# Four transformer blocks on one core: probs times V in joint units, a timed order for layer 0, a fused tail

## The reference, cut to what matters

```
x: (4, 512, 256) float32; cond: (4, 256)
layer 0: x += proj(attn(film(rmsnorm(x))));  one head of 256;  x += mlp(film(rmsnorm(x)))
layer 1: 16 heads of 16, q and k normalised to length 1 and scaled; adaptive shift, scale and gates
layer 2: 16 heads, layernorm with adaptive shift, scale and gates
layer 3: 16 heads, layernorm, adaptive gamma and beta; x += proj(attn); out = x + ln(x)*gamma + beta, no mlp
mlp: 256 -> 1024, gelu, -> 256
```

## Time and profile before

| what | us |
|---|---|
| median of 3 runs | 1274.11 |
| lowest and highest | 1271.5, 1274.75 |
| the profiled execution, its own time | 1271.56 |
| its span in the trace | 1269.8 |
| busy: PE, DVE, ACT, POOL | 1146.6, 779.8, 834.5, 538.0 |

### The profile page before, as it was taken

How to read it: one execution, slowest core, us unless ns; L and a number is a source line. 1 busy time by engine, 2 the same in 40 slices (tenths; PEclk the granted TensorE clock), 3 DMA queues, 4 the chain that set the end, 5 groups by cost and what they waited for, 6 DMA issues and landing times.

```text
span 1269.8 us, 20478 instructions
## 1 busy us (share of the span) xinstructions
PE 1146.6 (90%) x6868; PEld 718.8 (57%) x6868; DVE 779.8 (61%) x1587; ACT 834.5 (66%) x1471; POOL 538.0 (42%) x484
## 2 busy tenths in 40 slices
PE   4879889658999899899999999999999999999993
PEld 2667767634565465555664655656656656545532
DVE  4342332657558558658567467486674765888863
ACT  2563627315776766777876868678868687687771
POOL 2454447500444433443445545335544354354143
PEclk8989999858999999999999998999999999999987
DMA  6010000050430320332312423123331232242400
GB/s 213 9 34 1 26 1 17 1 96 5 101 80 26 67 57 12 61 74 43 60 26 47 89 63 70 34 45 69 63 52 34 36 61 52 44 92 46 82 26 17
DMA packets 40999, 64.52 MB, mean 51 GB/s; under 512 B 11816, under 2 KB 26920, under 8 KB 40896
## 3 DMA queue, kind: packets, MB, share of 16 engines
q1 hardware_dynamic: 40896, 63.21, 24.5%
HBM read 22.90 MB, written 2.12 MB: 20 GB/s over the span
## 4 chain that ended last, share of the span: by engine, by line
PE 66%; DVE 12%; issue 6%; ACT 6%; POOL 4%; SPq 4%; DMA 2%; ACTq 0%; POOLq 0%; DVEq 0%
PE ring L557 11%; PE AVB L644 11%; PE ring L631 10%; PE ring L558 10%; PE ring L559 10%; PE ring L621 5%; DVE m L1043 4%; SPq L519 3%; DVE stats L950 2%; PE ring L594 2%; PE ring L669 2%; PE ring L664 2%; POOL gT_l L1125 2%; ACT probs L812 1%; POOL X L1164 1%
## 5 line engine op out<-in xcount | busy, mean ns | idle before, releaser
L1043 DVE TENSOR_REDUCE m<-ring 128x1 f32<-128x512 f32 x768 | 480.7, 680 | 110.3 <-PE ring L621 92.0
L812 ACT ACTIVATE probs<-ring 128x512 f32<-128x512 f32 x768 | 406.3, 612 | 188.2 <-PE ring L621 163.0
L621 PE MATMUL ring<-SK,SQ 48*128 48x512 f32 x768 | 299.8, 471 | 25.6 <-DMA SK<-kl 16.4
L631 PE MATMUL ring<-SQ,SK 49*128 49x512 f32 x768 | 273.6, 448 | 13.2 <-DMA SQ<-cT 4.4
L631 PEld LDWEIGHTS ring<-SQ,SK 49*128 49x128 f32 x768 | 128.5, 190 | 226.2 <-issue 91.7
L644 PE MATMUL AVB<-probs,V 128*32 128x512 f32 x1536 | 211.2, 618 | 0.8 <-issue 0.8
L1125 POOL TENSOR_TENSOR gT_l<-gT_f,gT_h 128x512 fp32r<-128x512 f32 x96 | 122.1, 1287 | 155.5 <-ACT gT_h L877 152.5
L621 PEld LDWEIGHTS ring<-SK,SQ 48*128 48x128 f32 x768 | 131.2, 192 | 64.3 <-ACT probs L812 38.7
L1120 POOL TENSOR_TENSOR postT_l<-postT_f,postT_h 128x512 fp32r<-128x512 f32 x56 | 71.5, 1282 | 150.6 <-ACT postT_h L860 74.5
L557 PE MATMUL ring<-w_h,gT_h 128*128 128x256 f32 x384 | 110.5, 288 | 1.9 <-POOL gT_l L1125 0.9
L558 PE MATMUL ring<-w_l,gT_h 128*128 128x256 f32 x384 | 107.0, 279 | 0.0
(11 more groups left out here) (154 smaller groups left out, 2002.3 us busy)
## 6 DMA issues: line engine op xcount, KB each, us to landing
SQ<-qh SPq DMA_DIRECT2D x192, 64.0 KB, 2.3
SK<-kh SPq DMA_DIRECT2D x192, 64.0 KB, 2.3
SQ<-ql SPq DMA_DIRECT2D x96, 64.0 KB, 2.3
SK<-kl SPq DMA_DIRECT2D x96, 64.0 KB, 2.3
raw<-in_w SPq DMA_DIRECT2D x20, 256.0 KB, 2.8
...
```

The source lines that it names most:

```text
L621: mm = pe.matmul(o[:, :], SQ[a % 4][r:r + KS, n // 2, c * P:(c + 1) * P], SK[a % 4][r:r + KS, n // 2, :], start=True, stop=True)
L631: mm = pe.matmul(o[:, :], SK[a % 4][r:r + KS + 1, n // 2, c * P:(c + 1) * P], SQ[a % 4][r:r + KS + 1, n // 2, :], start=True, stop=True)
L812: act.activation(probs[:, n % PROBS, :], bank(kind, a, i)[:, :], ACT.Exp, scale=SCALE[layer(unit_job(a))]).then_inc(done["scores"], 1)
L1043: nc.vector.tensor_reduce(m16[:, a % 2, col:col + 1], bank(kind, a, i)[:, :], AX_X, ALU.max, negate=True).then_inc(done["max"], 1)
```

## The change

It rewrites the making of the list and some steps:

- Two ticks form one unit of the list. PAIR (layers 1 and 2) and PAIR_LAST (layer 3) say how: p6 is the next six of the 16 products, A both `av` steps of the two ticks before, 0 and 1 the rest of the first and of the second tick. A `shift` stands ahead of the rest of its tick.
- `probs` has 12 slots; `qk` lies over `gT_h`, with waits (READ_BEFORE) of gelu for the last q or k transposes and of qktok for the last fc2.
- Layer 0 and the step to layer 1 get a time for every step too (SINGLE, SINGLE3, FFN0, FFN2, FFN3, FIRST, LEAD_IN, MAXIMA); in the step, hT2, fc1 and fc2a of job 3 stand among LEAD_IN and MAXIMA, and its fc2 at ticks 0.9 and 1.95 of the first window. The times of the other tables are moved by up to 2 ticks.
- At the start (EARLY) DVE makes high and low of the three `split_qkv` and the low part of hT1 of job 0; 12 matmuls on a constant tile (WARM) stand ahead of all work of PE.
- Low parts of oT2 and av0: ACT writes the rounded value only, DVE makes the low part from PSUM in one instruction.
- proj of layers 0 and 3 (`direct`): POOL adds the bias to X ahead of it (`bias`), DVE adds PSUM to X.
- Last job: oT2, proj and bn_stats go by halves of the tokens; `base` (POOL) and `centre` (DVE) are new, and `final` is one DVE instruction per tile. In layer 3 the sum column of V is 16, so the scale of 1/16 goes with the reciprocal.

```diff
-PROBS = 8
+PROBS = 12
-CUT = (6, 6, 6, 8, 6, 8, 8, 6, 6, 4, 4, 2, 8, 6, 2, 4)
-CUT_LAST = (6, 6, 4, 6, 4, 2, 4, 6, 2, 4, 4, 4, 4, 8, 6, 8)
+SINGLE = {"stat1": (-17.1,), "norm1": (-15.95,), "hT1": (-9.6, -9.24), "q": (-7.06, -3.56), "k": (-6.4, -3.25),
+          "v": (1.2, 3.47), "scores0": (0.36, 0.71, 1.78, 2.13), "soft0": (2.49, 2.84, 3.56, 3.91),
+          "pT0": (7.11, 7.47, 7.82, 8.48), "av0": (11.53, 12.19), "proj": (12.96, 13.21), "stat2": (13.97,),
+          "norm2": (14.93,), "bias": (1.5,)}
+FFN0 = {"hT2": (17.07, 17.17), "fc1": (20.72, 21.08, 21.43, 21.79, 24.53, 24.89, 26.67, 27.02), "gelu": (22.14, 27.38),
+        "fc2a": (25.76, 26.11), "fc2": (30.12, 32.28)}
+LEAD_IN = {"stat1": (-17.86,), "norm1": (-16.36,), "hT1": (-12.27, -11.62), "qktok": (-9.69, -9.55, -8.95, -8.51),
+           "qkss": (-9.39, -9.15, -8.71, -8.47), "qkroot": (-8.22,), "v": (-7.78, -6.6), "qkrs": (-7.93,),
+           "qknorm": (-7.49, -7.34, -7.19, -6.95), "q": (-6.46, -6.12), "k": (-6.31, -6.02),
+           "stack": (-5.87, -5.72, -5.58, 2.2)}
+MAXIMA = (-5.2, -4.55, -4.53, -4.38, -4.24, -4.23, -4.09, -3.67, -3.53, -3.38, -3.23, -3.09, -2.79, -2.5, -2.35, -2.2, -1.32, -1.23, -1.23, -1.13, -1.04, -0.74, -0.39, -0.25)
+SHIFT = -1.42
+FFN3 = {"hT2": (7.93, 8.27), "fc1": (10.07, 10.22, 10.36, 10.51, 13.94, 14.09, 14.24, 14.39), "gelu": (10.66, 14.53),
+        "fc2a": (12.33, 13.21), "fc2": (16.9, 17.95)}
+PAIR = ("p6 A p6 0 p4 1", "p6 A p6 0 p4 1", "p6 A p6 0 p6 1", "p6 A p6 0 p4 1", "p6 A p6 0 p4 1", "p6 A p6 0 p4 1", "p6 A p6 0 p6 1", "p6 A p6 0 p4 1")
+PAIR_LAST = ("p6 A p8 0 p4 1", "p6 A 0 p4 1", "p6 0 1 A", "0 p6 A p6 1", "p6 A p6 0 p4 1", "A p6 0 p2 1", "p6 A p6 0 p4 1", "p4 0 p6 1 A")
...
+def multi_window(w, work):
...
+    for t in range(0, TICKS, 2):
+        pairs, rest = [], []
+        for x in (t, t + 1):
...
+            shift = [("shift", u - 1, 0)] if v % TT == 0 and u - 1 < UNITS * JOBS else []
+            rest.append(shift + [s for at, s in work if x <= at - TICKS * w < x + 1])
+        n = TICKS * w + t
+        av = [("av", x // TT, x % TT) for x in (n - 2, n - 1)] if n > TICKS * BATCH else []
+        plan += in_order((PAIR if layer(w) < LAYERS - 1 else PAIR_LAST)[t // 2], pairs, av, rest)
...
+            pe.wait_ge(warm_ready, 1)
+            for _ in range(WARM):
+                pe.matmul(ring[RING - 1][:, :], SK[0][:, 0, 0:P], SK[0][:, 0, :], start=True, stop=True)
...
-                    for dst in (postT_f[:, i, :], postT_h[:, i, :]):
-                        ins = act.activation(dst, bank(kind, a, i)[:, :], ACT.Identity,
-                                             bias=colv[:, 0, C_V + i:C_V + i + 1])
-                    ins.then_inc(hi_in[kind], 1)
+                    act.activation(postT_h[:, i, :], bank(kind, a, i)[:, :], ACT.Identity,
+                                   bias=colv[:, 0, C_V + i:C_V + i + 1]).then_inc(hi_in[kind], 1)
...
+                elif kind in ("oT2", "av0"):
+                    dve.wait_ge(hi_in[kind], nth(kind, a, i))
...
+                        ins = nc.vector.scalar_tensor_tensor(out=postT_l[:, i, :], in0=bank(kind, a, i)[:, :],
+                                                             scalar=colv[:, layer(a), C_V + i:C_V + i + 1],
+                                                             in1=postT_h[:, i, :].bitcast(F32), op0=ALU.add, op1=ALU.subtract)
...
+                elif kind == "final" and a == JOBS - 1:
+
+                    dve.wait_ge(done["centre"], i + 1)
+                    dve.wait_ge(rstd2, nth("stat2", a))
+                    dve.wait_ge(done["base"], i // 2 + 1)
+                    nc.vector.scalar_tensor_tensor(out=tok2[:, i, :], in0=tok2[:, i, :], scalar=rstd[:, 1, i:i + 1],
+                                                   in1=tmp[:, i, :], op0=ALU.mult, op1=ALU.add).then_inc(final_dve, 1)
...
+                elif kind == "proj" and direct(a) and a < JOBS - 1:
...
+                    nc.vector.tensor_tensor(x, bank(kind, a, i)[:, :].rearrange("p (t d) -> p t d", t=2), x, ALU.add
+                                            ).then_inc(done[kind], 1)
```

More of the change, by code:

```diff
@@ new lines @@
+ATTN = {"oT1": (17.35, 17.51, 17.52, 17.53), "oT2": (18.25, 18.61), "proj": (19.15, 19.9), "stat2": (21.0,),
+        "norm2": (22.5,)}
+FFN = {"hT2": (23.6, 23.91), "fc1": (25.15, 25.16, 25.17, 25.18, 29.5, 29.51, 29.52, 29.53), "gelu": (25.19, 29.54),
+       "fc2a": (27.95, 29.5), "fc2": (30.8, 31.35)}
+FFN3 = {"hT2": (7.93, 8.27), "fc1": (10.07, 10.22, 10.36, 10.51, 13.94, 14.09, 14.24, 14.39), "gelu": (10.66, 14.53),
+        "fc2a": (12.33, 13.21), "fc2": (16.9, 17.95)}
+OUTPUT = {"gatefix": (17.9,), "final": (22.6, 24.0, 26.55, 28.8), "store": (24.45, 27.05, 28.85, 32.0), "bias": (17.95,)}
@@ new lines, in timed @@
+def timed(table, j):
+    return [(TICKS * j + at, (kind, UNITS * j + i if kind == "stack" else j, 0 if kind == "stack" else i))
+            for kind, times in table.items() for i, at in enumerate(times)]
+def around(j):
+    if not multi(j):
+        return [s for s in timed(SINGLE if j < BATCH - 1 else SINGLE3, j) if s[1] not in FIRST] + timed((FFN0, FFN0, FFN2, FFN3)[j], j)
+    steps = timed(LEAD_IN, j) if j == BATCH else timed(COSINE if layer(j) == 1 else QKV, j)
+    if j == JOBS - 1:
+        return steps + timed(LAST, j)
+    return steps + timed(ATTN, j) + timed(FFN if layer(j) < LAYERS - 1 else OUTPUT, j)
@@ new lines, in lead_in, with layer_steps @@
+def lead_in():
+    u = UNITS * BATCH
+    steps = [(TICKS * BATCH + at, ("max", u + n // 16, n % 16)) for n, at in enumerate(MAXIMA)]
+    return steps + [(TICKS * BATCH + SHIFT, ("shift", u, 0))]
+def layer_steps(l):
+    if l == 0:
+        return [(at, s) for table in (FIRST, NEXT1) for s, at in table.items()]
+    steps = []
+    for kind, times in (FOR_LAYER if l < LAYERS - 1 else FOR_LAST).items():
+        ahead = kind in ("load_mod", "modrow", "mod", "load_gate", "load_qkv", "split_qkv")
+        for i, at in enumerate(times):
+            if kind not in ("modrow", "mod", "load_mod") or i < mod_rows(l + 1):
+                steps.append((TICKS * BATCH * l + at, (kind, BATCH * l + i, 0) if kind in ("gatecast", "vones") else (kind, l + ahead, i)))
@@ L252 @@
     if _s[0] in ("proj", "fc2a", "fc2"):
+        if _s[0] == "proj" and direct(_s[1]):
+            continue
         _tiles = (2 * _s[2], 2 * _s[2] + 1)
@@ L257 @@
 PIECES = [s for s in PLAN if s[0].startswith("split")]
+EARLY = [("split_qkv", 0, i) for i in range(3)] + [("hT1", 0, i) for i in range(CH)]
+WARM = 12
+READ_BEFORE, _read, _other = {}, {}, False
+for _s in PLAN:
+    if _s[0] in ("gelu", "qktok") and _s[2] == 0:
+        READ_BEFORE[_s] = _read.get("fc2" if _s[0] == "qktok" else "q")
+        assert _read.get("open", _s[0]) == _s[0], _s
+        _read["open"] = _s[0]
+    if _s[0] == "fc2":
+        _read["fc2"] = _s
+    if _s[0] in ("q", "k") and layer(_s[1]) == 1 or _s == ("modrow", 0, 1):
+        _read["q"] = _s
+    if _s[0] == "fc2" and _s[2] == 1 or _s[0] in ("q", "k") and _s[2] == 1 and layer(_s[1]) == 1 and _other:
+        _read.pop("open", None)
+    if _s[2] == 1 and _s[0] in ("q", "k"):
+        _other = not _other
 def nth(kind, a, i=0):
@@ L549, in claim @@
                     k, b, m = USES[n - RING]
-                    freed = {"proj": y1, "fc2a": done["fc2a"], "fc2": y2, "scores0": exp0}.get(k, hi_in.get(k))
-                    pe.wait_ge(done[k] if freed is None else freed, nth(k, b, m))
+                    if k == "proj" and not direct(b):
+                        pe.wait_ge(y1, nth(k, b, m) - 2 * BATCH)
+                    else:
+                        freed = {"hT1": hi_in["hT1"], "hT2": hi_in["hT2"], "fc2": y2, "scores0": exp0}.get(k, done.get(k))
+                        pe.wait_ge(freed, nth(k, b, m))
                 return ring[n % RING]
@@ L713, in _ @@
             for kind, a, i in PLAN:
-                if kind.startswith("split"):
+                if kind.startswith("split") and (kind, a, i) not in EARLY:
                     n = PIECES.index((kind, a, i))
```

352 lines of the change are left out of this document (165 added, 187 removed), and 7 rows, old and new, of tables (FIRST, START).

## The result

The changed kernel takes **1267.25 us** (median of 20 runs, 1260.99 to 1271.43), beside 1272.95 for 20 runs of the kernel before. The ratio is **0.9956**, 95% interval [0.9944, 0.9968]: faster by 0.4%. I had predicted 1186 (1148 to 1232). The direction held and the size did not: 5.7 us came where 87 were expected.

The account below looks back on a forecast made before the run. The prediction took PE to set the end nearly everywhere, in four different ways. Its terms summed to -88, so 1183.6 us for the profiled execution and, with 2.6 for the median, 1186 (own range 1165 to 1208; stated with the result as 1148 to 1232).

Parts of the forecast that it names:

- the shift's wait: Layers 1 to 3: with fewer products behind the shift, its DMA chain falls short by up to 2 us; +8 us.
- Start and tail: Start: shorter wait for the first hT_l, -5 us; tail: fewer passes and work by halves, -9 us (-5 to -12).
- Layer 0, -18: Layer 0: PE's waits for norm2 before hT2 go nearly whole, clock gains 4, 2 given back; -5 to -28 us.
- The step and the first window: Step to layer 1 and its first window: moved mlp work 15, wait before q 4, clock 8; -27 us (-10 to -45).
- the first rival: Whole kernel: evacuation by ACT and DVE is the bound, work leaving PE returns as waits; 1227 us, chance 0.25.
- Joints, -16: Layers 1 and 2: 64 joins of two `av` save 0.25 us each; -16 us (0 to -42).
- Banks, -8: Layers 1 and 2: the new order makes fewer late banks, 1 us per window; -8 us, bounded by 0 and 47.
- the third rival: Windows of layers 1 to 3: shifts behind the joint `av` hold up PE; 1300 us at 2.6 us each, chance 0.05.
- Layer 3, -5: Layer 3: 32 joins give 8 us, DVE gets 6 more of low parts, ACT loses copies; -5 us (+6 to -14).
- Low parts elsewhere, 0: Outside layer 3: 24 more low parts on DVE, 18 us, hidden beside PE; POOL's saving is off the path; 0 us.
- The signs: Among them: layer 0 tok waits at most 3 us, first scores at 245 to 260, its window 80, later ones 80 to 81.
- Evacuation (1227): The first rival, whole kernel: emptying PSUM through ACT and DVE is the bound; -47 us, 1227 us, chance 0.25.

Follow-up runs that it names:

- hole_empty: The changed kernel with the mlp of job 3 back in the first window of layer 1 instead of the hole before it: 1262.8 us, ratio 0.9925.
- old_times_all: The changed kernel with the order and times of the kernel before in layers 1 to 3: 1246.6 us, ratio 0.9801 to the kernel before.
- best_empty: The changed kernel with layer 3's old order and times, and the mlp of job 3 back in layer 1's first window: 1240.0 us, ratio 0.9774.
- join_only: `old_times_all` with the `av` of each two ticks joined into one run of 16 matmuls: 1279.3 us, ratio 1.0088 to the kernel before.
- experiment 4: The run `join_only` against `old_times_all`, both traces split by what ran and by clock level: 1279.3 us beside 1246.6.
- pool_low: The changed kernel with the low parts of oT2 of jobs 4 to 14 back on POOL and ACT writing twice: 1284.5 us, ratio 1.0096.

## Why the prediction was wrong, by its steps

Predicted -88 for the profiled execution, measured -6.6. Of the 81 that are missing 14 lie in layer 0, 18 in the step with the first window, 22 in windows 5 to 11 (the -24 of windows 5 and 6, joints, banks and the shift's wait) and 30 in layer 3; the tail gave 3 more than expected.

**Start and tail: right.** -4.9 and -12.1 beside -5 and -9, the tail just past its far end of -12. The reasons hold as well. The wait for hT_l fell by 3.6, and the tail's four last instructions take 1.67 us; DVE, the kernel after:

```profile
1256.98 1.67 DVE L1028 SCALAR_TENSOR_TENSOR tok<-X,mv,gates 128x256 f32<-128x256 f32 x4
1258.85 1.67 DVE L1036 SCALAR_TENSOR_TENSOR tok<-tok,rstd,tmp 128x256 f32<-128x256 f32 x4 [0.19 <-DVE tok L1028]
```

**Layer 0, -18: the waits were read right, what comes back behind them was not.** The wait for tok fell by 11.1, and up to `scores0` of job 3 layer 0 is 16.6 shorter. But the prediction's stretch ends with v of job 4, and by that cut it gained 4.2, less than the near end of 5. Behind `scores0` of job 3 PE has 303 matmuls instead of 273 (22 that stood ahead of it before, and the 8 transposes of hT2 of job 3), waits 3.1 us for the tok of that hT2, and is 6.8 us at the lower clock instead of 0.2. With the mlp of job 3 left in window 4 (`hole_empty`) this stretch takes 54.6 us instead of 60.1, and layer 0 gains 10.1. The -18 gave back 2 for what is late next; the runs show 7 (`hole_empty`) and 12.

`old_times_all` and `best_empty` give what start, layer 0, step, first window and tail are worth together without the losses behind them: 0.9801 and 0.9774, 25 and 29 us less than before.

**The step and the first window: -27, measured -9** (137.3 to 128.3 us from the end of v). The -4 for the wait before q came: 8.2 to 3.9. Two statements failed. The chain of the hole "stays as long as it was": the moved mlp lengthens it. The moved steps stand in one list with the chain and every engine takes them in that order; 20 maxima that took 12.05 us now come in batches of 7, 5 and 4 with holes between, so the first `scores` came 3.4 later behind the first `max`, and with hT2 in front of the chain too they are at 268.9 where `hole_empty` has them at 263.0. And "so there is room for the whole 18" in the window: from `hole_empty` to the kernel after PE's busy time there falls by 13.0 us (88.15 to 75.17), the window by 2.8. I took PE, busy in 91.4 of 98.7 us, for its bound. What is removed from PE there returns as waits, as the first rival said, but for DMAs (5.4 for SK<-kl and 5.3 for SQ<-cT of 15.4 idle) and not for ACT and DVE. The other 5 us of the window's 8 come without the moved mlp. The clock did rise in the hole, 0.55 to 0.82, and fell in the window, 0.90 to 0.83; no 8 us of it can be seen.

**Joints, -16: too large a price, and the wrong sum.** A join saves 0.15 us and not 0.25, so the 56 of windows 5 to 11 give 8.4 and the 64 of the term 10. What I left out is what the join does to the stretches around it. Added alone to the old order it costs 33 us (`join_only`), about half of it by more time at the lower clock, the rest by waits and later products. The forecast priced a switch and kept the clock and the waits of every other stretch. The Trainium skill (TensorEngine Tiling (Array Packing), Key Properties) says that a change of tiling mode drains TensorE. The 0.15 agrees in kind; the sum of such drains was no measure of the change.

**Banks, -8, and the shift's wait, +8.** Neither showed in the time. PE's waits for SQ<-cT sum up to 7.4 us in the whole execution, 4.4 before, so the third rival did not occur. Fewer late banks did come: in w5 to w11 the weight loads of `scores` waited for a maximum of DVE's 31.3 us before and 2.1 after.

```profile
PEld ring L631 <- DVE m L1043: 31.3, 46, 1.7
...
PEld ring L624 <- DVE m L1090: 2.1, 5, 0.4
```

The windows are no shorter for it. DVE waited longer for the bank's products, 172.6 us where it was 92.0; the kernel after, groups by line:

```profile
L1090 DVE TENSOR_REDUCE m<-ring 128x1 f32<-128x512 f32 x768 | 478.8, 682 | 188.2 <-PE ring L614 172.6 <-PE ring L624 15.2
```

I read it so that PE gives out products later, in lumps, and that it isn't DVE that holds PE.

**Layer 3, -5, measured +24.8 with window 12.** By the same split as in experiment 4, before and after in w12 to w15. At full clock the products take 0.242 us each instead of 0.209, x 422 = +14; the `av` 0.120 instead of 0.129, x 411 = -3.5; the rest +2. The low intervals are 42.1 us instead of 10.9; at the full-clock paces of before the same matmuls would have taken 25.7 and 6.8, so +12. Sum +24. The record has 37.5 us at the lower level instead of 10.2, at most 14 of the 24.8; the rest is products that start later, with PE idle 17.5 us instead of 9.1. Such a stretch in order of time, PE, the kernel after:

```profile
1118.79 0.31 PE L618 MATMUL ring<-ident,m 128*80 128x128 f32 x1
...
1120.26 3.21 PE L637 MATMUL AVB<-probs,V 128*32 128x512 f32 x16
1123.40 0.79 PE L624 MATMUL ring<-SQ,SK 49*128 49x512 f32 x1
```

The joint takes 3.14 us to the next product instead of 1.85. What failed is that my -5 had treated moved times of up to 2 ticks, and a new order, as free, because no instruction was added. (Its own terms, 8 of joins less 6 of low parts, give 2; the rest was ACT's copies, which it didn't price.) Each costs by itself: the new times 18.3 in the old order (13.7 of it those of q, k, v and the stacks), the new order 39.8 with the old times, both together 23.7. Which wait in the new order starts the loss, and why the clock falls there, stays open.

**Low parts elsewhere, 0: not contradicted in the old order; in the new one the move to DVE saves 17 us** (`pool_low`). A price worked out in the order of before need not hold in the order of after.

**The signs.** Of those named, the clock in the step (0.82) and the joint (1.85) came; the wait for tok just missed (3.1), and the first `scores` (268.9), its window (90.6) and the later ones (84.3) did not come.

**The rivals.** Evacuation (1227) had it right that work taken from the first window returns as waits, and wrong on whom PE waits for. None had a loss by the clock or by an order of times. Each term of all four cases was a gain or a wait; what was missing is a case in which the steady windows, 84 us each at a clock of 0.99, were already at their best and a new order could only lose.
